# The step sizes of a selective scan: a polynomial as three quartics, each two squares on ScalarE, in place of five quadratics

## The reference

```
xz = x @ in_proj_w;  x_in, z = split(xz)
xc = silu(causal_conv(x_in) + conv_b)              # 256 channels
ssm_out = xc @ x_proj_w                            # B (16), C (16), one column for dt
dt = softplus(ssm_out[..., -1:] @ dt_w + dt_b)     # the step sizes, [2048, 256]
A  = -exp(A_log)
y  = selective_scan(xc, dt, A, B, C, D_param)      # states decay by exp(dt * A)
out = (y * silu(z)) @ out_proj_w
```

## Time and profile before

| | us |
|---|---|
| median of 3 runs | 1544.56 (1542.48 to 1544.77) |
| the profiled execution | 1546.46, its span 1544.7 |
| TensorE busy | 1299.8 (84% of the span) |
| VectorE busy | 1242.2 (80%) |
| ScalarE busy | 1039.1 (67%) |
| GpSimd busy | 661.5 (43%) |
| VectorE's first scans, line 1426 | 157.5 in 128 instructions |
| ScalarE's decays, line 1176 | 85.1 in 128 instructions |

### The profile page before, as it was taken

The page is one execution under the profiler, slowest core; times in us unless marked ns, Lnnn a source line. Parts: engine busy times, 40 slices in busy tenths (PEclk is TensorE's granted clock), DMA queues, the critical chain, the costliest instruction groups (busy, mean ns, idle before and its releaser), DMA issues.

```text
span 1544.7 us, 22552 instructions
## 1 busy us (share of the span) xinstructions
PE 1299.8 (84%) x8408; PEld 504.2 (33%) x8408; DVE 1242.2 (80%) x1491; ACT 1039.1 (67%) x1821; POOL 661.5 (43%) x609
## 2 busy tenths in 40 slices
PE   4365669977974997887579999999999999999998
PEld 1111234333442443332222222222222222235963
DVE  0899998998999794576689999999999999933522
ACT  3542358765843753544249998999899988997653
POOL 0688867985886675653403113111211123111430
PEclk9675779998997998999669999999999999999999
DMA  8122223322421312322212101100010000010210
GB/s 224 64 79 71 72 58 102 82 62 70 102 68 48 96 55 49 61 47 51 33 54 50 29 29 48 22 2 2 2 22 2 2 2 19 6 29 10 75 31 28
DMA packets 63696, 75.71 MB, mean 49 GB/s; under 512 B 8633, under 2 KB 39226, under 8 KB 63458
## 3 DMA queue, kind: packets, MB, share of 16 engines
q1 hardware_dynamic: 62818, 72.70, 18.0%
q0 software_dynamic: 768, 1.57, 0.3%
HBM read 66.04 MB, written 8.21 MB: 48 GB/s over the span
## 4 chain that ended last, share of the span: by engine, by line
PE 45%; DVE 32%; issue 9%; POOL 7%; ACT 5%; DMA 1%; SPq 1%; DVEq 0%; POOLq 0%; ACTq 0%
DVE mx L1651 16%; PE PS L956 11%; PE PS L944 6%; DVE D L1440 5%; PE PS L913 4%; PE PS L727 3%; PE PS L736 3%; DVE PS L1426 3%; DVE PS L1432 2%; PE PS L1028 2%; PE PS L1043 2%; POOL D L1891 2%; PE PS L1064 2%; PE PS L1052 2%; PE PS L681 1%
## 5 line engine op out<-in xcount | busy, mean ns | idle before, releaser
L1313 ACT ACTIVATE aa<-PS 128x512 f32<-128x512 f32 x1024 | 551.5, 598 | 57.5 <-PE PS L944 46.6
L1651 DVE TENSOR_REDUCE mx<-PS 128x2 f32<-128x1024 f32 x480 | 552.2, 1215 | 8.0 <-PE PS L913 5.1
L956 PE MATMUL PS<-aa,D 128*32 128x256 f32 x4096 | 321.6, 391 | 1.6 <-ACT aa L1313 0.6
L944 PE MATMUL PS<-D 54*128 54x512 bf16 x1024 | 211.9, 390 | 9.4 <-ACT aa L1313 8.9
L913 PE MATMUL PS<-D 51*128 51x512 bf16 x960 | 189.9, 385 | 17.6 <-DVE mx L1651 16.8
L2005 POOL CAST n<-nm 4x512 bf16<-4x512 f32 x15 | 9.0, 602 | 446.2 <-ACT nm L1295 446.2
L1426 DVE TENSOR_TENSOR_SCAN PS<-PS,D 128x512 f32<-128x512 f32 x128 | 157.5, 1230 | 10.3 <-POOL D L1907 3.5
L1203 ACT ACTIVATE HB<-PS 128x512 f32<-128x512 f32 x144 | 84.8, 596 | 118.8 <-PE PS L736 118.2
L736 PE MATMUL PS<-xnT,f_w 128*128 128x512 f32 x288 | 156.6, 637 | 1.9 <-ACT HB L1203 1.2
L1176 ACT ACTIVATE D<-D,Am 128x512 f32<-128x512 f32 x128 | 85.1, 713 | 92.8 <-DVE D L1440 90.8
L727 PE MATMUL PS<-HB,f_w 128*128 128x512 f32 x288 | 146.2, 614 | 0.9 <-ACT FO L1207 0.9
(11 more groups left out here) (328 smaller groups left out, 1763.0 us busy)
## 6 DMA issues: line engine op xcount, KB each, us to landing
D<-bc SPq DMA_DIRECT2D x128, 256.0 KB, 3.7
GB<-gd SPq DMA_DIRECT2D x32, 256.0 KB, 4.5
D<-sc SPq DMA_DIRECT2D x72, 64.0 KB
aa<-in_L_ffn_W SPq DMA_DIRECT2D x9, 256.0 KB, 3.2
D<-in_L_ffn_W SPq DMA_DIRECT2D x9, 256.0 KB, 3.6
f_w<-in_L_ffn_experts_w SPq DMA_DIRECT2D x1, 2048.0 KB, 9.4
f_w<-in_L_ffn_experts_w SPq DMA_DIRECT2D x8, 256.0 KB, 6.2
aa<-gh SPq DMA_DIRECT2D x1, 2048.0 KB, 9.0
```

The costliest lines, as they stand in the source:

```text
L944: e.matmul(take_exp(s + hh), KS[64 * hh:64 * hh + 54, p, 128 * kb:128 * kb + 128], QP[64 * hh:64 * hh + 54, qc % 2, p, :], start=True, sto ...
L956: t = e.matmul(PS[32 * j:32 * j + 32, 7, cs], va[:, kb, 9 * h:9 * h + 32], Pt[K % 3][:, 512 * j + 256 * n:512 * j + 256 * n + 256], start= ...
L1313: e.activation(Pt[K % 3][:, c:c + 512], bank((s + hh) % 3), ACT.Exp).then_inc(S("e_free"), 1)
L1651: e.tensor_reduce(mx4[:, G % 2, b, 2 * pair:2 * pair + 2, c:c + 1], max_banks(m), AX.X, ALU.max).then_inc(freed(m)[0], 1)
```

## The change

The polynomial is now `LEAD * y` times three quartics, each written as `((y + a)^2 + b)^2 + c`: a square with bias `a`, a square of that with bias `b` (both on ScalarE), and on VectorE one add of `c` and product. The degree goes from 11 to 13. For each half of a chunk ScalarE has 6 squares in place of 5 and VectorE 4 instructions in place of 6. The second square of a pair waits for the first (a new wait of ScalarE for itself), and in `start` the first squares go to `SQ` and the second to PSUM. In the loop the generators of ScalarE and VectorE get shorter by as many yields as there are rounds less, so the step sizes of a half are done earlier, and GpSimd's two waits of 12 yields become 8.

```diff
-LEAD = 0.002037716592261226
-PAIRS = [(2.303017180067723, 0.5212684734404347), (1.7051292196135144, 1.388852113778505),
...
+LEAD = 1.856732948244197e-05
+QUARTICS = [(-1.490712003540543, 4.442426836762221, 7.623425359845395),
...
 # ScalarE, start
-                for r in range(5):
+                for r in range(3):
                     for g in range(2):
-                        w.wait_ge(S("const"), 7)
+                        n = 4 * r + 2 * g
+                        w.wait_ge(S("const"), 8)
                         w.wait_ge(S("s_exp"), g + 1)
+                        w.wait_ge(S("s_vv"), g + 1)
+                        w.wait_ge(S("s_sq"), n - 2)
+                        e.activation(SQ[g], yy2[g], ACT.Square, bias=cst[:, 2 * r:2 * r + 1]).then_inc(S("s_sq"), 1)
+                        w.wait_ge(S("s_sq"), n + 1)
                         if r:
                             w.wait_ge(S("s_pp"), 2 * r + g - 1)
-                        else:
-                            w.wait_ge(S("s_vv"), g + 1)
-                        e.activation(bank(7 - g), yy2[g], ACT.Square, bias=cst[:, r:r + 1]).then_inc(S("s_sq"), 1)
+                        e.activation(bank(7 - g), SQ[g], ACT.Square, bias=cst[:, 2 * r + 1:2 * r + 2]).then_inc(
+                            S("s_sq"), 1)
 # ScalarE, prolog of a chunk
-                    for r in range(5):
-                        if r >= 3:
-                            w.wait_ge(S("p_pp"), 5 * i + r - 1)
-                        e.activation(SQ[r % 2] if r else bank(7), ey[g], ACT.Square, bias=cst[:, r:r + 1]).then_inc(
-                            S("p_sq"), 1)
+                    for r in range(3):
+                        n = 6 * i + 2 * r
+                        w.wait_ge(S("p_sq"), n)
+                        e.activation(SQ[r % 2], ey[g], ACT.Square, bias=cst[:, 2 * r:2 * r + 1]).then_inc(S("p_sq"), 1)
+                        w.wait_ge(S("p_sq"), n + 1)
+                        e.activation(SQ[r % 2] if r else bank(7), SQ[r % 2], ACT.Square,
+                                     bias=cst[:, 2 * r + 1:2 * r + 2]).then_inc(S("p_sq"), 1)
                         yield from idle(2)
                     yield from idle(3)
 # VectorE, prolog of a chunk (start alike)
-                    for r, (_, im) in enumerate(PAIRS):
+                    for r, (_, _, more) in enumerate(QUARTICS):
...
-                        w.wait_ge(S("p_sq"), 5 * i + r + 1)
-                        e.scalar_tensor_tensor(out=bank(7), in0=SQ[r % 2] if r else bank(7), scalar=im * im,
+                        w.wait_ge(S("p_sq"), 6 * i + 2 * r + 2)
+                        e.scalar_tensor_tensor(out=bank(7), in0=SQ[r % 2] if r else bank(7), scalar=more,
 # GpSimd: six memsets of shifts in place of five, and
-                    yield from idle(12)
+                    yield from idle(8)
```

27 lines of the change are left out of this document (14 added, 13 removed).

## The result

| | before | after |
|---|---|---|
| median of 20 runs each, us | 1545.15 (1542.48 to 1549.2) | 1549.42 (1544.93 to 1553.58) |
| profiled execution, its span, us | 1546.46, 1544.7 | 1548.90, 1547.2 |
| VectorE busy, us | 1242.2 | 1235.0 |
| ScalarE busy, us | 1039.1 | 1046.2 |
| TensorE busy, us | 1299.8 | 1308.4 |

The ratio after to before is 1.0023 (95% interval 1.0014 to 1.0033): by it the change costs 3.6 us (2.2 to 5.1). Its range, 1540.5 to 1549.5, held the median of 1549.42 by 0.1 us, and its point was too low; "slower by over 0.2%", which had got 0.19, is what the ratio shows, though its interval begins at 0.14%. VectorE lost 7.2 us of work, as much as ScalarE gained (7.1).

A forecast was written before the change was run, and what follows sets the result against it. The prediction took VectorE to bound beside chunk 0's scan and TensorE the feed-forward stages; +0.8 - 1.76 + 0.7 + 0.7 + 0.7 = +1.2 us on 1544.56 gave 1545.8 us, own range 1543 to 1548, 8 in 10: 1540.5 to 1549.5.

The forecast's parts named there:

- What bounds: VectorE sets the pace in chunk 0's scan, TensorE in the feed-forward stages, where eight fewer VectorE products gain nothing.
- Rival 1: VectorE bounds throughout, so the kernel gets faster: 1538.8 us; chance 0.13.
- The start: First chunk's step sizes: six dependent ScalarE pairs make the chain longer, +0.8 us (bounds +0.4 to +1.0).
- Chunk 1: Chunk 1's step sizes beside chunk 0's scan: four VectorE products fewer at 0.44 us each, -1.76 us.
- Step 20: Chunk 0's epilog: the second square delays the normalizations and VectorE's copy of the gate logits, +0.7 us.
- Step 36: Chunk 1's epilog: normalizations 0.5 us later, gate matmuls still end before VectorE's copy at 348.68, so hidden.
- rival 3: TensorE's clock: slower gate matmuls, 1546.5 us (small form, 0.06); whole projection changing level, 2.8 us either way (large form, 0.05).
- FO: Both feed-forward stages: a pair before the copy into FO makes TensorE wait 0.73 us longer, +0.7 us twice.
- Steps 24 and 25: Pairs before a hidden activation delay it 0.73 us; TensorE's matmul just makes it: zero, 0.2 us to spare.
- rival 2: ScalarE's pairs before hidden activations stop TensorE in both feed-forward stages, 2.9 us on top: 1548.7 us; chance 0.14.
- Rival 4: The change takes no product off VectorE; given no chance.

The follow-up runs named there:

- chunks23_only: The kernel before with the quartics in the step sizes of chunks 2 and 3 alone; ratio 1.0020, +3.1 us (0.8 to 5.6).
- chunk1_only: The kernel before with the quartics in chunk 1's step sizes alone; ratio 0.9996, -0.6 us (-2.3 to +1.1).
- after_again: The changed kernel unaltered, run once more on another chip, against the kernel before there; 1558.31 us, ratio 1.0029, +4.5 us (3.1 to 5.9).
- start_only: The kernel before with the quartics in the first chunk's step sizes alone; ratio 1.0018, +2.8 us (1.1 to 4.6).
- extra_squares: The kernel before plus two unused ScalarE squares in half 0 of chunks 2 and 3 each; 1549.75 us against 1545.33, ratio 1.0033.

## Why the prediction was right in sign and too small

**What bounds (right).** VectorE bounds beside chunk 0 and TensorE in the feed-forward stages: the eight products that went from chunks 2 and 3 became VectorE's waits (6.00 for 3.77). Rival 1, VectorE bounds throughout, is out: chunks23_only got slower with less work on VectorE.

**The start (right).** +0.8 forecast, +0.97 in the traces. A pair took 0.74 + 0.63 = 1.37 us, forecast 1.35, and the last product began 0.11 us behind the end of its square, forecast 0.03. The timed +2.8 (1.1 to 4.6) of this part is more than the chain explains; that stays open.

**Chunk 1 (the step that failed).** The term -1.76 was sized right for the products and wrong for the path. The prediction said that ScalarE's squares "lie in its idle time: the stage leaves it 73 us free". Free time on average says nothing on one moment: before the first product, ScalarE's chain is projection, convolution, activations and then the pair, and the product that needs it comes at a fixed place in VectorE's order. The kernel before (order of time on both engines) had little to spare:

```profile
88.73 0.69 ACT L1164 ACTIVATE PS<-D,cst 128x512 f32<-128x512 f32 x1
...
90.24 0.67 DVE L1412 SCALAR_TENSOR_TENSOR PS<-PS,D 128x512 f32<-128x512 f32 x1
```

The square ended at 89.42, 0.8 us before the product began. The pair is 0.74 us longer, which would just have fitted; the projection, 1.07 us longer in after, did the rest, and VectorE waited 1.07 + 0.74 - 0.8 = 1.01. The same sum gives the others: 1.57 us in chunk1_only (1.63 longer), nothing in after_again (0.11 longer), and 0.2 in start_only with its single square (1.00 longer, 0.19 measured). So the term was worth between -0.2 and -1.7 us. But a slow projection delays the kernel before as well: between two executions with the same projection the pair can cost no more than its 0.74, and the term is -1.0 to -1.7. The whole piece up to copy 0, forecast at -1.06 (with step 20), was -0.61, -0.11 and -1.74 in the three traces against the one of before; start_only, with the same work in this piece as before, differs from it by -1.11 too.

**Step 20 (right at the place, hidden in this trace).** The normalizations began 1.38 us after the first square (204.58 to 205.96) in place of 0.62: +0.76, forecast 0.73. But VectorE's copy waited 2.46 in place of 2.40, since TensorE's transposes and gate matmuls behind them were together 0.8 us shorter in this execution (the latter 1.54 for 1.85). What the pair is worth shows when the traces are put side by side. The rest in this table is the time from the first scan to the normalizations, less the first pass of chunk 2's projection and less the wait at chunk 1's first product (all us).

| kernel | squares before them | chunk 1 | to the normalizations | first pass of chunk 2 | wait | rest |
|---|---|---|---|---|---|---|
| before | 1 | quadratics | 155.36 | 6.51 | 0 | 148.85 |
| start_only | 1 | quadratics | 154.84 | 5.65 | 0.19 | 149.00 |
| extra_squares | 2, independent | quadratics | 154.89 | 5.39 | 0 | 149.50 |
| chunks23_only | 2, a pair | quadratics | 154.71 | 5.10 | 0 | 149.61 |
| chunk1_only | 1 | quartics | 155.26 | 6.48 | 1.57 | 147.21 |
| after | 2, a pair | quartics | 155.16 | 6.20 | 1.01 | 147.95 |
| after_again | 2, a pair | quartics | 153.73 | 5.73 | 0 | 148.00 |

The pair costs 0.6 to 0.8 us at this place in every one, and the four products of chunk 1 save 1.6 to 1.8. What remains is TensorE's first pass of chunk 2, 5.10 to 6.51 us for the same matmuls: 1.4 us between executions, for which the prediction had no term, and which hid the pair in a comparison of two single traces.

**Step 36 ("hidden", failed in the trace, through rival 3).** It was +2.3 in the profiled execution and nothing in the second profile of the same kernel, as the projection before it took 6.24 or 3.70 us. Rival 3's large form was 2.8 us in either direction with 0.05; it came in the first profile. Its small form came in part: the gate matmuls of 346.44 took 1.88 us in place of 1.21 in after_again, chunks23_only and extra_squares, where TensorE had idled 3.01 to 3.15 us before the transposes in place of 2.72, but the copy behind them waited for nothing. The Trainium skill's page "TensorE: Matmul & The Clock Gate", section "What's actually happening", says that the number of matmuls at half rate differs between executions of the same kernel. The traces agree: the two profiles of the changed kernel have 6.24 and 3.70 us for the same eight matmuls of chunk 3, and 6.18 and 5.22 for those of chunk 1. The prediction used this page for one place and should have used it for the error of every term.

**FO (right).** +0.7 twice, measured +0.75 twice, and from copy 1 to copy 2 three kernels show it with +0.8 to +1.0. For the first of the two waits no piece shows it as cleanly.

**The sum.** With the terms as measured, +0.97 at the start, -0.1 to -1.7 up to copy 0, +1.5 for FO and 0 or +2.3 in step 36, it is +0.8 to +4.7 us, about +2.7 in the middle, where +1.2 was forecast. The timed +3.6 and +4.5 lie in its upper half. Between executions in which TensorE's passes are equally long the terms make less: 0.97 + 1.5 - 1.7 + 0.75 is 1.5 us, up to 0.74 more for the pair in chunk 1, and what the pair adds in step 36. The lower ends of the two timed intervals, 2.2 and 3.1, are at its edge or above it, so part of the loss is probably in no named term. That the clock's effects were priced in a rival and left out of the terms puts the error on the slow side (a late ScalarE can turn a slow projection into a wait, not into a gain); this is argued from the waits and not measured. The prediction's own range doesn't come out of its bounds either: they add up to 1542.4 to 1546.9 us, where it says 1543 to 1548, and the measured median is above both. That the wider range of 8 in 10 held it by 0.1 us is luck.

**Steps 24 and 25 (right).** No wait of TensorE for a hidden activation appeared; rival 2 did not come. Rival 4 neither: VectorE has 1475 instructions in place of 1491.

The Trainium skill's page "ScalarE: Activation LUTs", section "Rules for kernel authors", sends multiplications to VectorE. The rows: 0.712 us a square on ScalarE and 0.68 to 0.70 a product on VectorE, so neither engine is quicker. Whether moving them paid was decided by place: the same quartics gave +3.6 us where they stood and -5.4 us two yields later, and the same two yields with the quadratics -2.2.

## What to carry to other kernels

Before work is moved to an engine with idle time, look at what that engine does next: the added instruction costs what the one behind it is waited for, at each place, and a place that already shows a wait (2.40 us for the gate logits, 0.46 for FO) is the first to look at. When a change takes work off the bound engine and the time doesn't fall, shift the new work by a slot or two before giving it up. And where the traced effect is a few microseconds in 1545, cut the trace at fixed milestones, and take more than one trace: the unchanged tail alone moved by 5 us, and one pass of eight matmuls by 1.4 to 3.0 with the clock.

## What the runs showed of the hardware

- On ScalarE a dependent square starts 0.74 us after the one it needs, an independent one 0.61 to 0.63; into PSUM it takes 0.67 to 0.69 us, into SBUF 0.70 to 0.73.
- Eight matmuls of 512 columns, the same code after the same wait, took 3.70 to 6.74 us, between TensorE's two levels, 2.4 and 1.2 GHz; two profiles of one kernel had 6.24 and 3.70 at the same place. The granted clock was 0.59 over the 6.24 in after and 1.00 over the 3.70 in before.
- TensorE and VectorE stopped together for about 3.5 us in the attention, and ScalarE for part of it, on one chip only, in all three traces from it; before's median there was 1553.11 us against 1545 to 1547 on the others.
